# One-core Trainium2 kernel: x loads ahead of acc stores, sums of four pairs a group later, last blocks two steps a group, W and x in 4 KB rows

## What is computed

```python
s = einsum('bn,hln->bhl', x, beta)
ssq = einsum('bn,hln->bhl', x * x, beta * beta)
fm = 0.5 * sum(s * s - ssq, axis=-1)
y = fm + x @ W.T + b
```

## Time and profile before

| | |
|---|---|
| median of 3 runs | 797.54 us (797.26 to 799.69) |
| the profiled execution's own time | 796.32 us |
| its span | 794.5 us |
| mean granted TensorE clock | 0.991 of full speed |
| busy: PE / DVE / ACT / POOL | 776.8 / 555.4 / 410.4 / 366.8 us |

### The profile page before, as it was taken

The page is one execution under the profiler, slowest core; times in us unless marked ns, Lnnn a source line. Parts: engine busy times, 40 slices in busy tenths (PEclk is TensorE's granted clock), DMA queues, the critical chain, the costliest instruction groups (busy, mean ns, idle before and its releaser), DMA issues. The chain is left out here.

```text
span 794.5 us, 9817 instructions
## 1 busy us (share of the span) xinstructions
PE 776.8 (98%) x3382; PEld 637.2 (80%) x3382; DVE 555.4 (70%) x646; ACT 410.4 (52%) x564; POOL 366.8 (46%) x328
## 2 busy tenths in 40 slices
PE   8999999799999999999999999999999999989998
PEld 5887878588888888888888888888888888867886
DVE  6899467875766666666666665766576656688985
ACT  5665355455555655555555555556555545542330
POOL 0134174446554654455346545653555365423443
PEclk9999999899999999999999999999999999989999
DMA  9596963075624561466046515641663256338934
GB/s 335 218 381 279 338 207 94 16 291 170 219 110 145 180 227 51 146 212 212 26 153 218 208 32 185 228 157 45 222 210 121 75 197 219 132 82 314 387 123 154
DMA packets 66738, 145.35 MB, mean 183 GB/s; under 512 B 4864, under 2 KB 41728, under 8 KB 64384
## 3 DMA queue, kind: packets, MB, share of 16 engines
q1 hardware_dynamic: 66688, 144.72, 51.3%
HBM read 102.76 MB, written 41.94 MB: 182 GB/s over the span
## 5 line engine op out<-in xcount | busy, mean ns | idle before, releaser
L443 PE MATMUL bank<-t_hi,s_hi 128*128 128x512 f32 x1116 | 437.9, 392 | 12.4 <-ACT r L593 9.6
L447 PE MATMUL bank<-t_lo,s_hi 128*128 128x512 f32 x1124 | 439.5, 391 | 0.2 <-DVE t_lo L690 0.2
L449 PE MATMUL bank<-t_hi,s_lo 128*128 128x512 f32 x1116 | 435.9, 391 | 0.0
L443 PEld LDWEIGHTS bank<-t_hi,s_hi 128*128 128x128 f32 x1116 | 210.9, 189 | 60.6 <-ACT r L593 10.8
L447 PEld LDWEIGHTS bank<-t_lo,s_hi 128*128 128x128 f32 x1124 | 212.3, 189 | 44.3 <-DVE t_lo L690 0.7
L449 PEld LDWEIGHTS bank<-t_hi,s_lo 128*128 128x128 f32 x1116 | 210.8, 189 | 44.0
L953 POOL TENSOR_TENSOR r<-r 128x512 f32<-128x512 f32 x70 | 109.9, 1571 | 270.4 <-ACT r L605 270.4
L816 DVE TENSOR_REDUCE sums<-cs 128x128 f32<-128x1024 f32 x128 | 155.4, 1215 | 74.3 <-ACT cs L624 69.6
L800 DVE TENSOR_TENSOR cs<-bank,r 128x512 f32<-128x512 f32 x70 | 48.4, 691 | 87.2 <-PE bank L449 86.9
L957 POOL TENSOR_TENSOR cs<-r 128x512 f32<-128x512 f32 x70 | 92.6, 1323 | 23.3 <-issue 18.1
L949 POOL TENSOR_TENSOR acc<-acc,bias_all 128x128 f32<-128x128 f32 x128 | 58.1, 476 | 85.2 <-DMA acc<-acc_kept 85.2
(11 more groups left out here) (53 smaller groups left out, 354.8 us busy)
## 6 DMA issues: line engine op xcount, KB each, us to landing
s_hi<-s_hi_kept SPq DMA_DIRECT2D x30, 896.0 KB, 5.0
s_lo<-s_lo_kept SPq DMA_DIRECT2D x30, 896.0 KB, 6.8
t_lo_in<-beta_p SPq DMA_DIRECT2D x16, 1024.0 KB, 7.2
s_lo_in<-x_p SPq DMA_DIRECT2D x16, 512.0 KB, 5.1
acc_kept<-cs SPq DMA_DIRECT2D x16, 512.0 KB, 5.4
acc<-acc_kept SPq DMA_DIRECT2D x64, 128.0 KB, 5.3
acc_kept<-acc SPq DMA_DIRECT2D x64, 128.0 KB, 1.8
s_hi_kept<-s_hi SPq DMA_DIRECT2D x8, 896.0 KB, 6.7
```

The source lines that it names most:

```text
L443: nc.tensor.matmul(to, s_hi[:, slot, s_op, cols], hi[:, k, :], start=start, stop=False, skip_group_check=True)
L447: nc.tensor.matmul(to, s_hi[:, slot, s_op, cols], lo[:, k, :], start=False, stop=False, skip_group_check=True)
L449: return nc.tensor.matmul(to, s_lo[:, slot, s_op, cols], hi[:, k, :], start=False, stop=stop, skip_group_check=True)
```

## The change

1. `SUMMED_IN` and `SPLIT_IN` follow the rule for all groups: 14, 15, 72 and 73 are summed in 12, 13, 70 and 71 and get their low part in 13, 14, 71 and 72. For this, group 72 gets a place for low parts, between r5 and o11, and its sums (for 74) come ahead of the row sums of 71.
2. SyncE issues an x load of a group in `PREPARED` right after the load of `acc` and of blocks, ahead of the store of `acc`. The groups in which this happens stay (11, 12, 69, 70, 71).
3. The blocks of pass 9 are prepared in groups 65 to 68: steps 1, then 2 and 3, 4 and 5, 6 and 7.
4. W and x lie in DRAM so that a whole block of W, or a whole pair of x, is 4 KB in a row for each partition. B11 comes in one load, and so does pair 1. The four first products of TensorE (`first_product`) do the products with the high part of x first and wait for its low part only then.

The host's reordering of the arrays changes to match. The diff, cut to its core:

```diff
 PREPARED = [2, 3, 4, 5, 6, 7, PAIRS + 6, PAIRS + 7] + list(range(FIRST_Q, GROUPS))
 
 SUMMED_IN = {g: g - 2 for g in PREPARED}
-SUMMED_IN.update({PAIRS + 6: PAIRS + 3, PAIRS + 7: PAIRS + 4, FIRST_Q: FIRST_Q - 3, FIRST_Q + 1: FIRST_Q - 2})
 SPLIT_IN = {g: g - 1 for g in PREPARED}
-SPLIT_IN.update({PAIRS + 6: PAIRS + 4, PAIRS + 7: PAIRS + 5, FIRST_Q: FIRST_Q - 2, FIRST_Q + 1: FIRST_Q - 1})
 
 
 def order_of(n):
...
     n, i = g // PAIRS, g % PAIRS
     if n == 0:
         return {2: [1], 3: [2], 4: [3, 4], 5: [5], 6: [6], 7: [7]}.get(i, [])
+    if n + 1 == Q_PASS:
+        return {1: [1], 2: [2, 3], 3: [4, 5], 4: [6, 7]}.get(i, [])
     return [i] if i and n < Q_PASS else []
 
...
 
         @block.sync
         def _(sp):
-            def load_first(op, loaded, ks=slice(0, KP)):
-
-                sp.dma_start(t_hi_in[:, 1, op, ks, :], w_p[op][ks].rearrange("k p c -> p k c")
-                             ).then_inc(loaded, 16)
+            def load_first(op, loaded):
+
+                sp.dma_start(t_hi_in[:, 1, op, :, :], w_p[op]).then_inc(loaded, 16)
 
...
 
             def load_x(g):
-                blocks = x_at(g)[:, 0:4, :].rearrange("p (a b) c -> p a (b c)", a=2)
-                sp.dma_start(blocks, x_p[pair_of(g)].rearrange("a p c -> p a c")).then_inc(x_loaded[slot_of(g)], 16)
-
-            def load_x_part(pair, part, loaded):
-                blocks = s_lo_in[:, pair, 2 * part:2 * part + 2, :].rearrange("p b c -> p (b c)")
-                sp.dma_start(blocks, x_p[pair][part]).then_inc(loaded, 16)
+                blocks = x_at(g)[:, 0:4, :].rearrange("p b c -> p (b c)")
+                sp.dma_start(blocks, x_p[pair_of(g)]).then_inc(x_loaded[slot_of(g)], 16)
+
+            def load_x_part(pair, blocks, loaded):
+                sp.dma_start(s_lo_in[:, pair, blocks, :].rearrange("p b c -> p (b c)"),
+                             x_p[pair][:, 256 * blocks.start:256 * blocks.stop]).then_inc(loaded, 16)
 
...
                 sp.wait_ge(c21_added, count(g))
                 sp.dma_start(out[rows + P:rows + 2 * P, 0:COLS], f[:, 1, 0:COLS]).then_inc(stored, 16)
 
-            load_x_part(0, 0, x0_front_loaded)
-            load_first(B11, b11_loaded[0], slice(0, 1))
-            load_first(B11, b11_loaded[1], slice(1, 2))
-            load_x_part(0, 1, x0_rest_loaded)
-            load_x_part(1, 0, x1_loaded)
-            load_x_part(1, 1, x1_loaded)
+            load_x_part(0, slice(0, 2), x0_front_loaded)
+            load_first(B11, b11_loaded)
+            load_x_part(0, slice(2, 4), x0_rest_loaded)
+            load_x_part(1, slice(0, 4), x1_loaded)
...
                         store_q(n)
                         sp.wait_ge(q_stored, 16 * CHUNKS)
                     load_blocks(n + 1)
+
+                to = g + HALF - 1
+                if to in PREPARED:
+                    sp.wait_ge(p4_made, count(g - 1))
+                    if n == 1:
+                        sp.wait_ge(s_stored[slot_of(to)], 32)
+                    load_x(to)
                 if g == FIRST_MAIN:
                     store_v(g - 1)
                     load_acc(g)
...
                     store_acc(g - 1)
                 if i == 0 and n + 1 < Q_PASS:
                     store_q(n)
-                if 1 <= i <= HALF:
-
-                    to = g + HALF - 1
+                if 1 <= i <= HALF and to not in PREPARED:
                     sp.wait_ge(p4_made, count(g - 1))
-                    if n <= 2 and (n == 1 or slot_of(to) < 2):
-                        sp.wait_ge(s_stored[slot_of(to)], 64 if n == 2 or slot_of(to) >= 2 else 32)
-                    if to in PREPARED:
-                        load_x(to)
-                    else:
-                        load_s(to)
+                    if n == 1 or (n == 2 and slot_of(to) < 2):
+                        sp.wait_ge(s_stored[slot_of(to)], 64)
+                    load_s(to)
                 if n == 1 and i >= 6:
                     store_s(g)
-                if n + 1 == Q_PASS and i > HALF:
-                    sp.wait_ge(p4_made, count(g - 1))
-                    load_x(g + HALF - 1)
             for g in range(FIRST_Q, GROUPS):
...
                                    t_lo[:, n % 2, t_op, :, :], k, start and k == 0, k == KP - 1, ready)
                 return made
 
-
-            pe.wait_ge(s_lo_ready, 1)
-            whole(0, BANK_A, A11, B11, True)
-            pe.wait_ge(s_lo_ready, 2)
-            whole(0, BANK_D, A21, B11, True)
-            pe.wait_ge(s_lo_ready, 3)
-            whole(1, BANK_A, A11, B11, True)
-            whole(1, BANK_D, A21, B11, True)
+            def first_product(g, place, s_op, x_split):
+
+                hi, lo = t_hi[:, 0, B11, :, :], t_lo[:, 0, B11, :, :]
+                pe.wait_ge(s_hi_ready, x_split)
+                for k in range(KP):
+                    cols = slice(k * P, (k + 1) * P)
+                    pe.wait_ge(t_hi_ready, t_split_place(0, B11, k))
+                    nc.tensor.matmul(bank(g, place), s_hi[:, g, s_op, cols], hi[:, k, :],
+                                     start=k == 0, stop=False, skip_group_check=True)
+                    pe.wait_ge(t_lo_ready, t_split_place(0, B11, k))
+                    nc.tensor.matmul(bank(g, place), s_hi[:, g, s_op, cols], lo[:, k, :],
+                                     start=False, stop=False, skip_group_check=True)
+                pe.wait_ge(s_lo_ready, x_split)
+                for k in range(KP):
+                    nc.tensor.matmul(bank(g, place), s_lo[:, g, s_op, k * P:(k + 1) * P], hi[:, k, :],
+                                     start=False, stop=k == KP - 1, skip_group_check=True)
+
+
+            first_product(0, BANK_A, A11, 1)
+            first_product(0, BANK_D, A21, 2)
+            first_product(1, BANK_A, A11, 3)
+            first_product(1, BANK_D, A21, 3)
             for g in range(DIRECT):
...
 
             act.wait_ge(x0_front_loaded, 16)
             split_x(0, slice(0, 2))
+            act.wait_ge(b11_loaded, 16)
             for k in range(KP):
-                act.wait_ge(b11_loaded[k], 16)
                 split_high(0, B11, slice(k, k + 1))
             act.wait_ge(x0_rest_loaded, 16)
             split_x(0, slice(2, 4))
-            act.wait_ge(x1_loaded, 32)
+            act.wait_ge(x1_loaded, 16)
             split_x(1, slice(0, 4))
...
                 dve.wait_ge(r25_added, i + 1)
                 nc.vector.tensor_tensor(r5[:, :], bank(g, BANK_D), r5[:, :], ALU.add).then_inc(r257_added, 1)
+                if i == 0:
+                    for other in groups_for(SPLIT_IN, g):
+                        split_s(other)
                 dve.wait_ge(p2_made, count(g))
                 dve.wait_ge(f_loaded[i], 16)
                 nc.vector.tensor_tensor(f[:, 0, 0:COLS], bank(g, BANK_A), f[:, 0, 0:COLS], ALU.add
                                         ).then_inc(o11_added, 1)
+                for other in groups_for(SUMMED_IN, g):
+                    sum_s(other)
                 if i == 0:
                     sum_rows(g - 1)
-                for other in groups_for(SUMMED_IN, g):
-                    sum_s(other)
                 dve.wait_ge(p3_made, count(g))
                 dve.wait_ge(f12_added, i + 1)
...
     arrays = {
-        "x_p": blocks[:, [0, 1, 3, 2]].reshape(PAIRS, 2, 2, P, KP * P).transpose(0, 1, 3, 2, 4)
-                                      .reshape(PAIRS, 2, P, 2 * KP * P),
+        "x_p": blocks[:, [0, 1, 3, 2]].transpose(0, 2, 1, 3).reshape(PAIRS, P, 4 * KP * P),
         "beta_p": columns[:, :, ::-1].reshape(CHUNKS, P, 4, KP, COLS),
-        "w_p": w_columns[::-1].reshape(4, KP, P, COLS),
+        "w_p": w_columns[::-1].reshape(4, KP, P, COLS).transpose(0, 2, 1, 3),
         "bias": b.reshape(1, H),
```

More of the change, by code:

```diff
@@ L163, in fm_layer @@
         x_loaded = [sem(f"x_loaded{i}") for i in range(HALF)]
-        b11_loaded = [sem(f"b11_loaded{i}") for i in range(KP)]
+        b11_loaded = sem("b11_loaded")
         b21_loaded = sem("b21_loaded")
```

## The result

The changed kernel takes **793.05 us** (median of 20 runs, 790.66 to 795.75) against 796.19 for the kernel before (18 of its 20 runs on the same chips): a ratio of **0.996, 95% interval [0.995, 0.997]**. Two runs of the kernel before, of 862.73 and 865.03 us, were slow ones and are left out. The changed kernel is faster by about 3.1 us, where 11.5 were forecast, and outside the range. The profiled execution took 792.64 us, span 790.9 against 794.5, which is 3.6 us less.

A forecast was written before the change was run, and what follows sets the result against it. TensorE's chain of matmuls was taken as the bound. Terms -8.0 - 6.9 - 0.6 + 0.3 + 2.3 + 1.4 = -11.5 us gave 784.8 profiled, forecast 786.0 us as median; range of 8 in 10: 782.8 to 789.6.

The forecast's parts named there:

- the first of group 12: Group 12: ScalarE's split of pair 14 begins at 136.1, its low half is ready at 145.65, wanted at 145.75.
- 2.4 us for a set: Group 13: VectorE's four sums of pair 15 take 2.4 us, as a set beside one GpSimd operation had.
- -8.0 for group 13: Group 13: the old stall behind the copy of r1, 5.6 us idle and 2.4 at lower clock, goes.
- -6.9 for group 71: Group 71: the old stall, 4.0 us idle and 2.9 slow, goes.
- +0.3 at r1 of group 14: Group 14: r1 is ready at 151.3, a little after TensorE wants it, costing 0.3 us.
- +2.3 at the start of group 15: Start of group 15: a new stall of 2.3 us, as the low half of pair 15 is ready at 157.9.
- +1.4 at group 73: Group 73: the 0.9 us lost behind r5 grow by 0.7 to 1.6, taken as 1.4 us.
- -0.6 for the start: Kernel start: the fourteenth matmul comes at 10.7 instead of 11.31, a gain of 0.6 us.
- VectorE isn't late: Rival, 13%: sums meet no GpSimd operation, new stalls shrink to 1 us and 0.7, giving 782.5 to 783.5.
- one stall stays: Rival, 4%: a late load or unseen wait brings 7 to 8 us of one old stall back, giving 793.
- Port contention: Rival, 3%, groups 13, 71, 72: every set of sums takes 5.1 us, the kernel is 3 us slower, 800.6.
- The clock falls again: Rival, 17%: new idle times at groups 15 and 73 lower the clock, 788.6 with one fall, 791.4 with both.

The follow-up runs named there:

- experiment 3: GpSimd's T4 sum of the next pass moved from group 13 to group 11, in the changed kernel: 790.54 us, ratio 0.9936 to the kernel before.
- experiment 5: VectorE's sums of s put ahead of r2 in the main groups, in the changed kernel: 788.05 us, ratio 0.9904 to the kernel before.
- experiment 1: The kernel before with only SyncE's order changed, x loads ahead of acc stores: 789.72 us, ratio 0.9925.
- experiment 2: The changed kernel with the old start and rows of W and x: 793.66 us; the kernel before with the new start and 4 KB rows alone: 795.21 us.

## Why the prediction was wrong

**The step that failed** is the first of group 12: "ScalarE's cast at 135.12 ends at 136.16, so the split of 14 begins at 136.1". It took the sums of pair 14 as done by then, and priced the contention only for pair 15, where T4 "is over by then". But the change puts the set of 14 just where the set of 15 had stood, behind r2 of group 12 and beside GpSimd's last quadrant and T4. The forecast had read 5.1 us for a set in this place, and did not price it again. It took 6.1 us where 2.7 would have done (133.43 to 136.1), so the split began at 139.52, 3.4 late. The forecast's own sign for this came too: the split of 15 begins at 153.67, and later than 150 was to mean that it was wrong. The low half follows at 150.06, not 145.65; 3.4 of these 4.4 us are the split's, 1.0 the acc update, which was stretched against the forecast's argument that nothing lengthens it there. TensorE waits at the start of group 14: +3.5 us, which had been put at nothing, "in time by a hair". Experiments 3 and 5 show it: taking T4 away, or taking the sums out from behind r2, brings 2.5 and 5.0 us back.

The 2.4 us for a set were too short as well. The set they were read from began 1.4 us late for its load, when GpSimd's last quadrant was nearly over. With the load early the same set takes 3.6 us (experiment 1, 125.09 to 128.65), and in the changed kernel those of 15, 72 and 73 take 3.1, 3.4 and 3.1. So the surcharge of 1.0 us for a set, which the forecast worked out and left out of its sum, was nearer.

The terms, one by one, in the profile (losses are starts of TensorE less 0.2275 us):

- -8.0 for group 13: 0.35 is left of it, right. But the reason ("the order of instructions" at the load) was right for group 71 only. In group 13 the load's part was 2.1 us (experiment 1), and VectorE's queue made the rest, so moving the work moved the stall.
- -6.9 for group 71: the stall is gone, right; from group 15 to 73 the kernel wins 5.6 us, with 0.9 lost at the end of it.
- +0.3 at r1 of group 14: 0.7 at 156.42.
- +2.3 at the start of group 15: 2.4, right by luck: with pair 14 late the set of 15 began 4.4 us late too, and TensorE was as late as its feeder.
- +1.4 at group 73: 2.8 behind r5 against 0.9 before is +1.9, and +0.9 at its start, which the forecast did not have: VectorE's low half of 73 took 3.08 instead of 2.01 beside GpSimd's output sums. Together 2.8, twice the term.
- -0.6 for the start: 0.6 to 0.9 in the runs of experiment 2, not clear of noise, and +0.3 in this profile.
- Groups 66 to 68 at 0, and no wait for a DMA: right.

The sum: 0.3 + (0.35 + 3.5 + 0.7 + 2.4 - 8.0) + (0.9 - 6.9) + 1.9 = -4.9 against the profile's -3.6. Of the 1.3 that remain, about 0.5 is the 0.1 us that each restart costs in its second interval (0.34 us from 163.13 to the next matmul, not 0.23; six restarts where one stood), the rest was not traced.

**The rivals.** "VectorE isn't late" and "one stall stays" did not come: VectorE was later, and both old stalls went. Port contention was the right mechanism, given 3% because it was asked to make the kernel slower in all sets at once. It needed only one set, and the set it struck was not among those priced. "The clock falls again" did not happen in the profiled execution, which kept it over 3.38 us of idle time. By the mean clocks it did in 18 of the 20, whose median lies only 0.9 us above the two others, too few to price a fall by. Where it fell in them no trace shows, but one case can be read. In the profile of the change without its start the same stall of 3.38 us was followed by a clock of 0.50 (window: stretch, its us, busy of PE, PEclk, DMA, GB/s),

```profile
150.50:154.00 3.50, 3.50 (x9) 0.50 0.00 0
```

and that kernel was hardly slower: its stall at group 15 shrank from 2.25 to 0.71 us, because VectorE's chain, not TensorE, set when group 15 began. A lower clock ahead of a stall comes out of the stall; where no such stall follows, as in group 73 of experiment 5, nothing gives it back.

## What to carry to other kernels

When work moves within an in-order queue, list what the other engines do in its new place, first of all what the instruction ahead of it releases; a template taken from the old place has the old neighbours in it. Ask of an idle time behind a late load how long the load itself held anyone (here 2.1 of 8.0 us lost): if the queue would have been as late, the stall moves along with the work. And run the parts apart: here one part alone beat the whole change, and moving the sums ahead of r2, one edit for four groups, brought 5.0 us, more than the whole change.

## What was not expected of the hardware

A small two-input VectorE operation of 0.41 us takes 1.5 beside a GpSimd operation of 1.3 us and 2.6 beside one of 2.6; large ones grow by about 1.1 us, from 2.01 to 3.1. GpSimd pays too: the r5 + r7 sum, 1.30 us elsewhere, took 2.28 where it stood beside VectorE's 1.2 us subtraction (sums first, 141.58), and an output sum 3.07 beside the low half of s (GpSimd's timeline of the changed kernel, group 72):

```profile
714.60 3.07 POOL L981 TENSOR_TENSOR t_lo_in<-t_lo_in,r 128x512 f32<-128x512 f32 x1
```

The same idle time of TensorE, 3.38 us ahead of the same matmul, left the clock at 1.00 in one kernel's profile and at 0.50 in another's; the same holds for 2.25 us at the start of group 15 (changed kernel and experiment 3). The length of the idle time alone did not decide it.
